# A decoder layer on one core: cross values formed once, masked keys as a mean, new step orders

## The reference, cut to what matters

```python
x = x + nystrom_attention(layernorm(x))        # 64 landmarks, pinv by 6 iterations
x = x + cross_attention(layernorm(x), ctx)     # 64 context keys per element, some masked
x = x + ffn(layernorm(x))                      # one of 8 experts per element, chosen from its last row
```

```python
V = x
for _ in range(6):
    KV = x @ V
    V = 0.25 * V @ (13 * I - KV @ (15 * I - KV @ (7 * I - KV)))
out = attn1 @ (pinv(attn2) @ (attn3 @ v))
```

```python
Q, K, V = query @ Wq.T + bq, ctx @ Wk.T + bk, ctx @ Wv.T + bv       # per element, split in heads
scores = jnp.where(mask == 0, -1e9, Q @ K.T / 4)
ctx_out = softmax(scores) @ V
x = x + ctx_out @ Wo.T + bo
```

## Time and profile before

| | |
|---|---|
| median of 3 runs | 1399.6 us (1397.81 to 1400.72) |
| profiled execution | 1397.8 us, its span from first to last instruction 1396.1 us |
| PE busy | 1355.2 us, 97% of the span |
| DVE busy | 1029.5 us, 74% |
| ACT busy | 667.0 us, 48% |
| POOL busy | 571.1 us, 41% |
| data moved | 53.18 MB, 38 GB/s on average |

### The profile page before, as it was taken

The page is one execution under the profiler, slowest core; times in us unless marked ns, Lnnn a source line. Parts: engine busy times, 40 slices in busy tenths (PEclk is TensorE's granted clock), DMA queues, the critical chain, the costliest instruction groups (busy, mean ns, idle before and its releaser), DMA issues.

```text
span 1396.1 us, 53472 instructions
## 1 busy us (share of the span) xinstructions
PE 1355.2 (97%) x23732; PEld 889.7 (64%) x23732; DVE 1029.5 (74%) x2194; ACT 667.0 (48%) x1230; POOL 571.1 (41%) x799
## 2 busy tenths in 40 slices
PE   6998999999999999999999999999999999999998
PEld 4756666666766767665666766666666656676555
DVE  3487887758786886878778686877868777898641
ACT  2424355454555546355554644555454544435652
POOL 6223444443626244362534436153353543417132
PEclk9999999999999999999999999999999999999999
DMA  8002010120201011020101101010110100001122
GB/s 285 1 3 95 3 63 3 45 75 3 66 5 51 20 38 33 3 66 5 51 20 37 34 3 58 13 51 20 37 34 3 52 2 19 18 4 39 25 77 65
DMA packets 40536, 53.18 MB, mean 38 GB/s; under 512 B 9698, under 2 KB 30450, under 8 KB 40306
## 3 DMA queue, kind: packets, MB, share of 16 engines
q1 hardware_dynamic: 31602, 41.37, 9.2%
q10 hardware_dynamic: 8704, 8.39, 1.8%
HBM read 37.16 MB, written 12.59 MB: 36 GB/s over the span
## 4 chain that ended last, share of the span: by engine, by line
PE 85%; DVE 5%; ACT 3%; issue 2%; POOL 1%; DMA 1%; DVEq 1%; POOLq 0%; SPq 0%; ACTq 0%
PE bank L1322 41%; PE bank L1575 8%; PE bank L1341 7%; PE bank L1331 7%; PE bank L1564 3%; PE bank L1530 2%; PE bank L1418 2%; PE bank L1397 2%; PE bank L1462 2%; PE bank L1543 2%; PE bank L1451 2%; ACT p3T L896 1%; PE bank L1385 1%; PE bank L1562 1%; PE bank L1424 1%
## 5 line engine op out<-in xcount | busy, mean ns | idle before, releaser
L778 POOL TENSOR_TENSOR b<-ut,eye 128x256 f32<-128x256 f32 x192 | 137.6, 733 | 498.6 <-DVE ut L1161 428.9
L940 ACT ACTIVATE az<-bank 128x320 f32<-128x320 f32 x192 | 67.5, 400 | 185.6 <-PE bank L1331 185.2
L1322 PE MATMUL bank<-xnT_a,wqkv 128*128 128x512 f32 x256 | 123.6, 609 | 0.3 <-ACT xnT_a L864 0.3
L1218 DVE RECIPROCAL oT_x<-bank 128x256 f32<-128x256 f32 x64 | 109.2, 1733 | 19.2 <-PE bank L1575 19.2
L1322 PE MATMUL bank<-w2e,hT 128*128 128x256 f32 x512 | 119.0, 386 | 1.5 <-ACT hT L1006 1.4
L1218 DVE RECIPROCAL oT<-bank 128x256 f32<-128x256 f32 x64 | 111.5, 1747 | 10.6 <-PE bank L1575 10.6
L1322 PE MATMUL bank<-xnT_c,w1e 128*128 128x512 f32 x256 | 117.0, 597 | 1.3 <-DVE m_x L1192 0.9
L1090 DVE TENSOR_REDUCE m<-bank 128x1 f32<-128x512 f32 x128 | 82.9, 680 | 38.5 <-PE bank L1418 36.9
L1322 PEld LDWEIGHTS bank<-w2e,hT 128*128 128x128 f32 x512 | 96.0, 192 | 16.9 <-issue 2.7
L896 ACT ACTIVATE p3T<-bank 128x512 f32<-128x512 f32 x128 | 66.7, 603 | 79.1 <-PE bank L1451 78.9
L959 ACT ACTIVATE pT_x<-bank,neg_bias 128x512 f32<-128x512 f32 x128 | 79.9, 696 | 29.8 <-PE bank L1564 28.8
(11 more groups left out here) (223 smaller groups left out, 2979.2 us busy)
## 6 DMA issues: line engine op xcount, KB each, us to landing
x_in<-in_x SPq DMA_DIRECT2D x16, 512.0 KB, 3.8
w1e<-in_W SPq DMA_DIRECT2D x16, 512.0 KB, 3.5
w2e<-w2o SPq DMA_DIRECT2D x16, 512.0 KB, 4.1
out<-base ACTq DMA_DIRECT2D x32, 256.0 KB, 2.1
row_e<-w2o_row SPq DMA_DIRECT2D x16, 128.0 KB, 4.6
hT<-in_W2T SPq DMA_DIRECT2D x2, 512.0 KB, 6.5
pT_x<-in_ctxT SPq DMA_DIRECT2D x1, 1024.0 KB
ctxT<-in_ctxT SPq DMA_DIRECT2D x16, 64.0 KB, 2.6
```

The costliest lines, as they stand in the source:

```text
L778: return g.tensor_tensor(b7[:, q, :], ut[:, q, :], eye[28 if it else 7][:].unsqueeze(1) .broadcast_to([P, 4, LM]), ALU.subtract).then_inc( ...
L1218: return v.reciprocal(oT[x][:, k, cols], tile(i, ("den" + x, k))[:, cols]).then_inc(dve_done, 1)
L1322: last = mm(dst, lhsT, rhs, start=(k == 0), stop=(k == len(pairs) - 1))
```

## The change

Seven things change.

1. **Masked keys.** The matmuls of L1539, with ones3, neg_col, neg_row and what made them, go. In their place DVE's kx writes into the masked columns of kxT the mean of the element's valid keys, so that a masked key can't give the row maximum. `neg_bias` still takes masked keys out of the exponent, and is now multiplied by whether the element has any valid key.
2. **Cross values.** vx is eight steps at the start, each for two elements at once, from ctx_all. DVE adds the bias into vx_all, which lies in pT_1; SP stores it (`vs`, eight times 128 KB) to a tensor in memory. Per element SP loads it back in block form (`vb`, two transfers of 64 x 8 runs of 64 bytes) once ox of the element before is done. The first e1 on ACT waits for the stores; ex waits for kx and vx; ox waits for the load.
3. **Constants.** The fusion's constants are issued right behind x, then one w2, then the first constants (a step of its own, `qc`), then the other w2's.
4. **FIRST** is a new table.
5. **TURN** is a new table; the store of an element (`out`) now lags four turns.
6. **LAST** is a new table.
7. The bias row's layout on the host follows that of the values.

No tile is held twice: vx_bd and x_in are single as before.

The diff, cut to its core:

```diff
@@ SP
-                    if i == 0:
-                        for dst, src in FIRST_CONSTS:
-                            sp.dma_start(dst, src).then_inc(first_consts_loaded, 16)
+                elif kind == "qc":
+                    for dst, src in FIRST_CONSTS:
+                        sp.dma_start(dst, src).then_inc(first_consts_loaded, 16)
...
-                elif kind == "ctx":
-                    if c := unmet(sp, "P", i - 1, ("vx",)):
+                elif kind == "vs":
+                    g = step[1]
+                    if c := unmet(sp, "D", 0, ("vx", g)):
+                        sp.wait_ge(dve_done, c)
+                    sp.dma_start(vx_dram[g * P:(g + 1) * P, :], vx_all[:, g]).then_inc(vx_stored, 16)
+                elif kind == "vb":
+                    if c := unmet(sp, "P", i - 1, ("ox", 0), ("ox", 1)):
                         sp.wait_ge(pe_done, c)
-                    sp.dma_start(ctxT[:], ctx_dram[:, :, i * LM:(i + 1) * LM]).then_inc(ctx_loaded, 16)
...
+                    for h in range(2):
+                        sp.dma_start(vx_bd[LM * h:LM * h + LM, :, DH * h:DH * h + DH],
+                                     vx_dram[i * LM:(i + 1) * LM, P * h:P * h + P].rearrange("c (a d) -> c a d", a=PAIRS)
+                                     ).then_inc(vx_loaded, 16)
@@ ACT, e1 and ex
+                    if x == "x":
+                        if c := unmet(act, "P", 0, ("kx", 0), ("kx", 1), *[("vx", g) for g in range(PAIRS)]):
+                            act.wait_ge(pe_done, c)
+                    else:
+                        if first(act, vx_stored, 16 * PAIRS):
+                            act.wait_ge(vx_stored, 16 * PAIRS)
@@ DVE, kx
-                        v.tensor_scalar(neg_row[:], mask_in[:], 0, neg_col[:], ALU.is_equal, ALU.mult)
+                        v.tensor_scalar(masked[:], mask_in[:], 0, None, ALU.is_equal)
                         v.tensor_scalar(neg_bias[:], mask_col[:], 0, -1e9, ALU.is_equal, ALU.mult)
                         v.drain()
+                        v.tensor_reduce(key_count[:], by_element(key_mask), AX.X, ALU.add)
+                        v.drain()
+                        v.tensor_scalar(some_key[:], key_count[:], 1.0, None, ALU.min)
+                        v.tensor_scalar(key_count[:], key_count[:], 1.0, None, ALU.max)
+                        v.drain()
+                        v.reciprocal(key_count[:], key_count[:])
+                        v.tensor_tensor(neg_bias[:], neg_bias[:], some_key[:], ALU.mult)
+                        v.drain()
...
                     for k in range(KD):
-                        last = v.scalar_tensor_tensor(kxT[:, k, g], tile(i, step, k)[:], bkx_col[:, k:k + 1],
-                                                      key_mask[:, g], ALU.add, ALU.mult)
+                        v.scalar_tensor_tensor(kxT[:, k, g], tile(i, step, k)[:], bkx_col[:, k:k + 1],
+                                               key_mask[:, g], ALU.add, ALU.mult)
+                    v.drain()
+                    for k in range(KD):
+                        v.tensor_reduce(key_mean[:, k, e], by_element(kxT[:, k, g]), AX.X, ALU.add)
+                        v.drain()
+                        v.tensor_tensor(key_mean[:, k, e], key_mean[:, k, e], key_count[:, e], ALU.mult)
+                        v.drain()
+                        v.tensor_tensor(by_element(masked_keys), by_element(masked[:, g]),
+                                        key_mean[:, k, e].unsqueeze(2).broadcast_to([P, 8, LM]), ALU.mult)
+                        v.drain()
+                        last = v.tensor_tensor(kxT[:, k, g], kxT[:, k, g], masked_keys, ALU.add)
@@ PE, vx and sx
-                    for r in range(2):
-                        last = chain(o[64 * r:64 * r + 64, 0:P],
-                                     [(ctxT[:, k, :], wv[:, k, r * P:(r + 1) * P]) for k in range(KD)])
+                    last = chain(o[:, 0:D], [(ctx_all[:, k, n * P:(n + 1) * P], wv[:, k, :]) for k in range(KD)])
...
-                    for j in range(4):
-                        r = slice(32 * j, 32 * j + 3)
-                        mm(tile(i, step, j)[:], ones3[r, :], neg_row[r, i * LM:(i + 1) * LM].unsqueeze(1)
-                           .broadcast_to([3, 8, LM]), start=True, stop=False)
@@ TURN, a few words of it
-    P.ox.0-3 A.e1.0.3-2 G.b7.1.0-2 P.iT.1-2 P.iZ.1-2 A.e1.0.2-2 D.wb.1.0-2 D.ox.0-3 G.kxbd-2 A.az.1.0-2
+    A.az.0.0-1 D.mx1.0.0-1 P.jT.0-1 D.ut.0.1-1 P.jZ.0-1 D.ut.0.0-1 D.uz.0.0-1 P.ox.1-2 D.uz.0.1-1 P.iZ.1-1
```

489 lines of the change are left out of this document (247 added, 242 removed), and 2 rows, old and new, of the table OPERANDS_FROM.

## The result

The changed kernel takes 1442.36 us (median of 4 runs, 1439.25 to 1445.22) against 1398.7 for the kernel before (4 runs, 1396.4 to 1400.72): a ratio of 1.0312, 95% interval 1.0279 to 1.0345. It is slower by 3.1%. The forecast was 1403, range 1388 to 1416; the result lies outside. The profiled execution took 1444.94 us, its span is 1443.2 us, at a granted clock of 0.991 of full speed on average.

What follows compares the result with a forecast made beforehand. The matrix engine PE was taken as the bound. Work -8.7, start -3.3, key block +4.7 and ten turns +11.5 gave +4.2, lowered to +3.7 for rounding: 1403 us from a median of 1399.6, range 1388 to 1416.

Steps and rivals of the forecast that it cites:

- The turn: One repeat of the loop's order table: 81.94 us before, forecast 82.1 after less PE work and more waits.
- term +1.15: New PE waits in a turn, behind j pairs and at s1: 1.5 us against 0.35 before, so +1.15 us.
- term -1.03: PE work leaving each turn, two sets of bias matmuls and the per-element values: 0.22 x 2 + 0.59 = 1.03 us less.
- Keys' mean: DVE's longer key blocks in element 0's iteration: PE waits 3.7 us at jZ.2, then 0.65 and 0.3; +4.7 us in all.
- Start: PE's first fusion matmul at 7.3 instead of 10.66 us, since the fusion's constants load first: -3.3 us.
- The small-run load: Per-element value load in 64-byte runs, estimated at 4.2 us, hidden before its use at ox.1: 0.
- FIRST and LAST: New order tables at the start and end, outside what is counted elsewhere: nothing, between -6 and +6 us.
- B: Covers behind the pairs hold, PE idle stays 0.35 us a turn: 1392 us, down to 1388; chance 0.35.
- C: DVE bounds from iT.0 to iT.2 of a turn, row maxima delaying ut or uz: 1414 us; chance 0.20.

Runs made afterwards that it cites:

- e1: Changed kernel with POOL's row additions (xr, x1b, base) as four instructions of 128x256 instead of one of 128x1024: 1415.2 us, ratio 1.0123.
- e2: Changed kernel with POOL's xr and x1b, whole, moved behind kbd in TURN and held until DVE has passed mT3 and mpx: 1421.87 us, ratio 1.0179.
- e5: All parts of the change (mean, values of all elements, constants first) put in the order tables of the kernel before: 1414.13 us, ratio 1.0124.
- e4: Kernel before without the mask matmuls of L1539, masked keys counting in the row maximum, so its output differs: 1394.24 us, ratio 0.9974.
- e11: Changed kernel with POOL's row additions split in four and the keys' mean left out, both together: 1408.91 us, ratio 1.0063.
- e3: Changed kernel with the mean of the valid keys left out of kxT, masked keys being zero there: 1439.72 us, ratio 1.0284.
- e9: Kernel before with fusion's constants first and the mean, in small steps in iterations of elements 0 and 1, replacing L1539's matmuls: 1401.1 us, ratio 1.0014.
- e12: Like e9, but the mean's small steps moved out of the iterations' early rounds, behind o1, lnB and y of elements 0 and 1: 1403.51 us, ratio 1.0028.
- e8: Kernel before with only the fusion's constants issued ahead of the first w2 and the first constants: 1395.79 us, ratio 0.9980.
- e10: Like e1, with two more matmuls of 128 columns in each ox, repeating products already formed: 1413.9 us, ratio 1.0103.

## Why the prediction was wrong

**The turn** is the step that failed: "+1.15. A turn is 81.94 - 1.03 + 1.15 = 82.1". It is 85.63. Two things were wrong in it, the first much the larger.

- *What was missing: 2.7 us a turn.* The step counted PE's covers and DVE's queue, and never laid POOL's order beside DVE's. POOL's xr and x1b now run back to back beside mp3, and DVE's tiny instructions wait each for the end of a POOL instruction. Measured: 24.6 us in nine turns. e1 takes away 2.65 us a turn and 27 us in all, e2 2.6 a turn; that is shown. Through a pair of long POOL instructions in FIRST it costs another 2.4 us (3.9 against 1.5 at mT1), and both dips of the clock in the nine turns (0.83 in 10 us, from 386 and from 476) follow it. The Trainium skill (SBUF — State Buffer, "Who interferes with whom") says that casts in a 2-port mode and operations with both inputs in SBUF share a port pair with GpSimd, and that whoever issues first has it "for the whole instruction", while `tensor_reduce` never contends. The trace agrees: 2.39 and 2.21 us beside POOL instructions of 2.36 and 2.34; whether this CAST runs in a 2-port mode, no run here shows by itself. By that rule and the order of the two engines these 2.7 us could have been forecast, and the profile before has every price: x1b's 2.4 us and mp3's four instructions.
- *What was sized too high: the saving.* Beside the lock, the forecast was 1.5 us of waits a turn. In the nine turns themselves (366.26 to 1136.95 us) PE is idle for 37.3 us, 12.7 beside mT3's, 1.4 a turn: the sum was right. The places were not. Only 1.3 us are released by uz; the others stand at s1 (the maxima that empty its banks, 2.9), at zT (2.7), and as issue gaps (3.7). Then the turn of e1 should be 82.1 and is 82.98. Its nine turns have PE idle for 14.4 us against 3.2 before, and busy for 732.5 against 734.4: +1.24 and -0.22 a turn. So the term +1.15 held, and the term -1.03 came out at -0.22. In the old orders less was lost of it: PE's busy time fell by 0.72 a turn in e5, and 0.43 of idle time came in, 0.36 of it at t3.1, ahead of which the values' eight matmuls had stood: these had been cover for that wait. In e4, 0.23 of 0.44 came back, with no new idle time. Two reasons are thus seen, lost overlap between neighbouring matmuls (0.33 for 0.44 at sx) and lost cover (e5); why the new orders lose 0.8 of the 1.03 was not tried apart.

**Keys' mean**, "+4.7 us". The one wait was sized well: 3.7 forecast at jZ.2, 3.3 measured. The whole is 6.3 us by e11 against e1, and 7.1 at element 0 in e3, of which 0.8 is the earlier first matmul. The waits behind the blocks were forecast; the lower clock behind the stall was not (1.35 us instead of 0.73 for jZ.2's matmuls alone). e9 and e12 price the mean in place of the matmuls at 5.3 and 7.7 us net in the old orders.

**Start**, "-3.3 us", forecast 7.3 for the first matmul. In the changed kernel's timeline:

```profile
8.39 4.18 PE L1361 MATMUL bank<-wfo,xnT_c 128*128 128x256 f32 x9 [8.39 <-DMA xnT_c<-in_W2T]
```

8.4, a gain of 2.3; in e8 it starts at 8.0 and the kernel gains 3.0. Over the profiled runs with the new orders it is 7.6 to 8.7. The step holds, a little oversized: the w2 that comes last is late, not the constants. The rate behind it took 2.5 us before the first byte, which no row shows: before, the core's DMA moved 173 GB/s from 2 to 3 us and 296 to 401 in each of the three after it.

**The small-run load**, "0". No PE step waits for a DMA at ox. The page of the changed kernel has each of its two transfers at 2.5 us, where 4.2 had been estimated for both together:

```profile
vx_bd<-vx SPq DMA_DIRECT2D x32, 32.0 KB, 2.5
```

**FIRST and LAST**, "at nothing, between -6 and +6". Element 3 is 19.7 us late, and the end gives 5.7 back. With the split and without the mean (e11) it is 7.5 us late. So these two and the clock dips that go with them hold 12.2 of the 19.7; the mean alone gave 5.1 (e11 against e1) to 10.6 (e3), the split 7.1 (e1), and e10, with the split and other dips, 3.4. The other 7.5 fits the eight vx steps (7.7 by the prediction's estimate); no run tried them apart. That this term was held to 6 either way made the range too narrow.

**The rivals.** B (covers hold) fell: 82.98 without the lock. C gave 1414, and a turn of 83 and more, by row maxima of DVE ahead of ut and uz. e1 stands at 1415, but with another cause: its waits for ut and uz sum to 0.4 us in nine turns. That the change is slower was forecast, but in part by luck: most of what makes it slower is the lock, which the forecast did not have. Its own terms miss by 12 us where the lock is all but gone (e1), and by 39 with it.

**The sum, as measured**, on the span: nine turns 24.6 of lock and 33.0 - 24.6 = 8.4 of other waits, of two turns at a clock of 0.98, and of a saving that did not come; start +19.7, end -5.7; together +47.0 of 47.1.

**Open.** Part of the 47 us is the clock: PE's busy time rose by 5.2 us, although by the prediction's sums its work fell by 8.7, and fell to 1354.7 in e1, whose mean granted clock was 0.998 against 0.991. How much the clock costs apart from the stalls ahead of it, no run separates. e11 has a turn of 83.30 against e1's 82.98 at a clock of 1.00 in each turn, so that difference is another one; it was not tried.

## What to carry to other kernels

When an order table changes, lay the engines beside each other that share something, not only those that wait for each other: a POOL instruction of 2.4 us next to a DVE instruction of 0.15 that PE waits for costs 2.2, and cutting the POOL instruction in four took 27 us off for an edit of three lines. Work taken off the engine that sets the time is worth its start-to-start time at most: its neighbours may have overlapped with it, and something behind it may have waited in its shadow; here about 4 of 7.0 us came back. Try each part alone in the old order first: one part, the order of the first transfers, was worth 3.0 us, and the mean cost more than the matmuls it replaced.

## What the runs showed of the hardware

- A DVE CAST and a DVE TENSOR_TENSOR of 128x8 out of SBUF took 2.39 and 2.21 us beside a POOL TENSOR_TENSOR of 128x1024, 0.76 and 0.59 beside pieces of 128x256, and 0.15 and 0.17 alone. The same two of 128x64 took 2.14 and 2.25 us beside the whole instructions. Two DVE reductions out of a bank (L1118) beside POOL's ksq, two instructions of 0.6 us, took 1.28 us together, no more than their usual 0.68 each.
- After stalls of PE of 2 to 8 us the granted clock read 0.64 to 0.85 in a stretch of 10 us (changed kernel at 90 and 150, e5 at 80 and 90). Not after every one: the same 2.7 us at mT3 left the clock at 1.00 in seven of the changed kernel's nine turns and in three of e3's, and the 3.3 us at jZ.2 left it at 1.00 in e2. And e9 had such a stretch behind waits of 1.5 and 1.0 us:

```profile
90.00:100.00 10.00, 9.02 (x216) 6.23 (x208) 9.30 (x19) 1.53 (x4) 1.53 (x3) 0.66 0.01 3
```

PE counts as 90% busy there, at half clock for most of it. A busy share alone hides this; the clock column shows it.
